# A conditioned low-rank linear kernel on one core: condition numbers read from DRAM for the first two tiles, and one residual sum and its loads moved in the opening

## What is computed

```python
y = jnp.einsum('bct,bcd->bdt', x, cond_weights[condition])
z = jnp.einsum('bsd,od->bso', y, W) + b
u = jnp.einsum('bsd,edr->ebsr', y, A)
m = jnp.einsum('ebsr,ero,e->bso', u, B, p_scores)
gamma = jnp.minimum(0.5 * norm(z) / (norm(m) + 1e-6), 1.0)
out = x + z + gamma * m
```

## Time and profile before

| what | value |
|---|---|
| median of three runs | 925.62 us (925.12 to 926.47) |
| the profiled execution | 925.62 us, of which the trace's span is 923.8 us |
| busy, share of the span | PE 99%, DVE 62%, ACT 39%, POOL 35% |
| PE's share of the chain that ended last | 93% |
| mean granted TensorE clock | 0.998 of full |
| data moved by DMA | 75.16 MB, 81 GB/s on average |

### The profile page before, as it was taken

The page is one execution under the profiler, slowest core; times in us unless marked ns, Lnnn a source line. Parts: engine busy times, 40 slices in busy tenths (PEclk is TensorE's granted clock), DMA queues, the critical chain, the costliest instruction groups (busy, mean ns, idle before and its releaser), DMA issues.

```text
span 923.8 us, 15176 instructions
## 1 busy us (share of the span) xinstructions
PE 911.9 (99%) x4884; PEld 786.3 (85%) x4884; DVE 575.9 (62%) x897; ACT 358.2 (39%) x695; POOL 319.5 (35%) x317
## 2 busy tenths in 40 slices
PE   8999999999999999999999999999999999999996
PEld 6888888888888888888888888888888888888885
DVE  5995656556565556565565655565655656555664
ACT  6653443324334333433343343334333433433342
POOL 0123443224433244432344332444323443324441
PEclk9999999999999999999999999999999999999999
DMA  8212221122221122211222211222112222122211
GB/s 292 81 70 95 81 85 69 47 94 94 71 93 46 71 94 75 90 66 50 94 94 71 93 45 73 94 71 94 61 56 94 94 71 93 40 77 94 72 46 68
DMA packets 32600, 75.16 MB, mean 81 GB/s; under 512 B 12745, under 2 KB 13770, under 8 KB 32586
## 3 DMA queue, kind: packets, MB, share of 16 engines
q1 hardware_dynamic: 32138, 74.43, 22.6%
q10 hardware_dynamic: 448, 0.56, 0.2%
HBM read 41.42 MB, written 33.55 MB: 81 GB/s over the span
## 4 chain that ended last, share of the span: by engine, by line
PE 93%; DVE 4%; DMA 1%; SPq 1%; issue 1%; ACT 0%; DVEq 0%
PE b_ps L853 36%; PE c_ps L853 18%; PE mix_ps L840 11%; PE u_ps L892 10%; PE m_ps L903 9%; PE a_ps L853 9%; DMA a_lo_raw<-in_L_ffn_A_dram 1%; SPq L266 1%; DVE w_lo L612 1%; DVE s_lo L642 0%; DVE y_lo L621 0%; DVE w_lo L576 0%; DVE w_lo_raw L595 0%; DVE w_lo_raw L581 0%; PE mix_ps L903 0%
## 5 line engine op out<-in xcount | busy, mean ns | idle before, releaser
L423 ACT CAST y_hi<-mix_ps 128x512 fp32r<-128x512 f32 x126 | 74.4, 592 | 309.3 <-PE mix_ps L840 309.3
L364 POOL TENSOR_TENSOR stats<-stats 128x1 f32<-128x1 f32 x32 | 18.8, 588 | 474.3 <-ACT squares L471 474.3
L642 DVE TENSOR_TENSOR s_lo<-s,s_hi 128x512 fp32r<-128x512 f32 x124 | 135.9, 1115 | 4.2
L840 PEld LDWEIGHTS mix_ps<-mixer,x_in 128*128 128x128 f32 x1008 | 122.2, 192 | 6.7 <-DMA x_in<-in_x_dram 1.0
L840 PE MATMUL mix_ps<-mixer,x_in 128*128 128x128 f32 x1008 | 122.9, 275 | 0.6 <-DVE y_lo L621 0.5
L436 ACT CAST s_hi<-s 128x512 fp32r<-128x512 f32 x124 | 76.6, 618 | 115.8 <-POOL s L338 93.7
L350 POOL TENSOR_TENSOR z<-z,x_in 128x512 f32<-128x512 f32 x61 | 79.2, 1299 | 116.7 <-ACT squares L452 116.7
L621 DVE TENSOR_TENSOR y_lo<-mix_ps,y_hi 128x512 fp32r<-128x512 f32 x126 | 86.4, 687 | 46.0 <-ACT s L429 39.6
L853 PE MATMUL b_ps<-w_hi,y_hi 128*128 128x512 f32 x256 | 100.1, 391 | 0.0
L853 PE MATMUL b_ps<-w_lo,y_hi 128*128 128x512 f32 x256 | 100.0, 391 | 0.0
L853 PE MATMUL b_ps<-w_hi,y_lo 128*128 128x512 f32 x256 | 99.6, 389 | 0.0
(11 more groups left out here) (120 smaller groups left out, 1842.5 us busy)
## 6 DMA issues: line engine op xcount, KB each, us to landing
x_in<-in_x_dram SPq DMA_DIRECT2D x64, 512.0 KB, 3.7
out_dram<-z SPq DMA_DIRECT2D x63, 512.0 KB, 2.7
w_lo_raw<-in_L_ffn_W_dram SPq DMA_DIRECT2D x8, 256.0 KB, 6.5
mixer<-in_L_cond_weights_dram SPq DMA_DIRECT2D x126, 16.0 KB, 2.1
w_hi_raw<-in_L_ffn_W_dram SPq DMA_DIRECT2D x6, 256.0 KB, 6.6
w_hi_raw<-in_L_ffn_W_dram ACTq DMA_DIRECT2D x2, 256.0 KB, 3.0
a_lo_raw<-in_L_ffn_A_dram SPq DMA_DIRECT2D x1, 512.0 KB, 7.9
b_lo_raw<-in_L_ffn_B_dram SPq DMA_DIRECT2D x1, 512.0 KB, 7.0
```

The costliest lines, as they stand in the source:

```text
L364: nc.gpsimd.tensor_tensor(stat(NORM_Z, 1), stat(Z_SQ, 1), half, ALU.pow).then_inc(norm_z_ready[1], 1)
L423: nc.scalar.copy(y_part(y_hi, r, h), source(h)).then_inc(y_hi_ready, 1)
L642: nc.vector.tensor_tensor(s_lo[:, n, :, :], s_raw(n), s_hi[:, n, :, :].bitcast(fp32), ALU.subtract).then_inc(s_lo_ready, 1)
L840: made = nc.tensor.matmul(source(h)[:, k, :], x_in[:, slot, (h * HC + k) * P:(h * HC + k + 1) * P], mixer[:, r, :], start=True, stop=True)
```

## The change

In the opening, the condition numbers of tiles 0 and 1 are no longer read from `cond_ids` in SBUF but straight from the input in DRAM; the DMA that fills `cond_ids` moves behind the loads of W12. SP and ACT therefore don't wait for it. ACT issues its small mixer DMAs and W11's first two chunks before the load of its activation table. The scaling of B by the scores moves from ACT to DVE. The bias difference `bias[:, 2]` is made later on DVE, between a split of T1 and the splits of S3 and S1. The square of z's upper half of tile 0 moves on ACT behind the squares of tile 1. The residual of tile 0 moves on DVE from before the splits of T4 to behind `add_p4_bias(1)`, and in SP's first half-step the load of tile 4 and of its mixers stands behind the loads of tile 5 and the store of tile 1, as in all later steps. Nothing inside the loop's steady part changes, save that `square_z11` names one semaphore less.

```diff
         def first_condition(engine, t, q):
             n = t * PER + q
-            return engine.value_load(cond_ids[0:1, n:n + 1], min_val=0, max_val=E - 1)
+            return engine.value_load(condition.rearrange("(o n) -> o n", o=1)[:, n:n + 1], min_val=0, max_val=E - 1)
...
-            sp.dma_start(cond_ids[:, :], condition.rearrange("(o n) -> o n", o=1)).then_inc(ids_loaded, 16)
             sp.dma_start(x_in[:, 0, :], x_tiles[0]).then_inc(x_loaded[0], 16)
             sp.wait_ge(mixer_zeroed, 1)
-            sp.wait_ge(ids_loaded, 16)
             sp.dma_start(first_mixer(0, 0), cond_block(first_condition(sp, 0, 0))).then_inc(mixer_loaded[0], 16)
...
             load_w(W12)
+            sp.dma_start(cond_ids[:, :], condition.rearrange("(o n) -> o n", o=1)).then_inc(ids_loaded, 16)
             load_w(W21)
...
-                    if first:
-                        sp.wait_ge(residual0_ready, 2)
-                        sp.dma_start(x_in[:, 0, :], x_tiles[4]).then_inc(x_loaded[0], 16)
-                        sp.wait_ge(mix_done, halves(2, 1))
-                        load_mixer(4, 0)
...
-                    if not first and not closing:
+                    if not closing:
                         sp.wait_ge(residual0_ready, 2 * p)
...
                 if not opening:
                     act.wait_ge(z12_squared, p)
-                    act.wait_ge(m_squared[1], p)
...
                 if opening:
-                    act.wait_ge(z12_squared, 1)
+                    act.wait_ge(z11_squared, 1)
...
-            act.dma_start(raw11[:, 0, :], w_blocks[W11][0]).then_inc(w_loaded[W11][0], 16)
+            act.wait_ge(mixer_zeroed, 1)
+            act.dma_start(first_mixer(0, 1), cond_block(first_condition(act, 0, 1))).then_inc(mixer_loaded[0], 16)
+            for k in range(2):
+                act.dma_start(raw11[:, k, :], w_blocks[W11][k]).then_inc(w_loaded[W11][k], 16)
+            act.dma_start(first_mixer(1, 1), cond_block(first_condition(act, 1, 1))).then_inc(mixer_loaded[1], 16)
             act.wait_ge(half_set, 1)
             nc.scalar.activation(table_out, half, ACT.Square).then_inc(table_loaded, 1)
-            act.wait_ge(mixer_zeroed, 1)
-            act.wait_ge(ids_loaded, 16)
-            act.dma_start(first_mixer(0, 1), cond_block(first_condition(act, 0, 1))).then_inc(mixer_loaded[0], 16)
-            act.dma_start(raw11[:, 1, :], w_blocks[W11][1]).then_inc(w_loaded[W11][1], 16)
-            act.dma_start(first_mixer(1, 1), cond_block(first_condition(act, 1, 1))).then_inc(mixer_loaded[1], 16)
...
-            act.wait_ge(bm_loaded, 16)
-            act.wait_ge(p_loaded, 16)
-            nc.scalar.activation(b_raw, b_raw, ACT.Copy, scale=p_col).then_inc(bm_scaled, 1)
...
-            square_z12(0, 0, z11_squared)
...
             square_m1(0, True)
+            square_z12(0, 0, m_squared[1])
...
+            dve.wait_ge(bm_loaded, 16)
+            dve.wait_ge(p_loaded, 16)
+            nc.vector.tensor_scalar(b_raw, b_raw, p_col, None, ALU.mult).then_inc(bm_scaled, 1)
             make_t3(0)
...
-            dve.wait_ge(z11_squared, 1)
-            dve.wait_ge(z12_squared, 1)
-            nc.vector.tensor_tensor(z0[:, 0, :], z0[:, 0, :], x_in[:, 0, :], ALU.add).then_inc(residual0_ready, 2)
             split_t(T4, 0)
...
             split_t(T3, 0)
             dve.wait_ge(bias_difference_ready, 1)
             add_p4_bias(1)
+            dve.wait_ge(z12_squared, 1)
+            nc.vector.tensor_tensor(z0[:, 0, :], z0[:, 0, :], x_in[:, 0, :], ALU.add).then_inc(residual0_ready, 2)
             split_t(T3, 1)
```

More of the change, by code:

```diff
@@ L735, in _ @@
             make_t1(1)
-            nc.vector.tensor_tensor(bias[:, 2, :], bias[:, 0, :], bias[:, 1, :], ALU.subtract
-                                    ).then_inc(bias_difference_ready, 1)
             dve.wait_ge(plain_done, 6)
@@ L772, in _ @@
             split_t(T1, 1)
+            nc.vector.tensor_tensor(bias[:, 2, :], bias[:, 0, :], bias[:, 1, :], ALU.subtract
+                                    ).then_inc(bias_difference_ready, 1)
             split_s(1, S3)
```

## The result

The changed kernel takes 942.56 us (938.20 to 942.97, four runs) against 925.4 us before: ratio 1.0173, 95% interval 1.0149 to 1.0196. It is slower by 17 us, where 11 were forecast; the time lies 2.6 us above the range. The profiled execution took 940.29 us, 2.3 less than the median.

The account below looks back on a forecast made before the run. PE was taken as the bound, busy without pause in the loop, so any standstill before it adds to the end. 9.1 us of stall and 1.9 of clock make 11.0 on 925.62: 936.6 us, range 933.0 to 940.0.

Parts of the forecast that it names:

- The stop before tile 4: PE waits for tile 4 and its mixers, so that mix starts at 66.0 instead of 56.44, 9.6 us later, 9.1 net.
- s: Cost of the scaling of B in DVE's list: 0.6 us, bounds 0.55 to 1.15.
- The landing: From the residual's end and tile 4's issue until its mixers have landed and PE can mix: 4.9 us.
- L: Time of one register load from DRAM, two per condition number: 0.8 us, between 0.28 and 1.3.
- d: How much later DVE's backlog begins, through SP's later DMA of A: 1.5 us, bounds 0 and 4.1.
- the forecast 61.1: End of tile 0's residual on DVE in us, from 59.03 + 0.6 + 1.5.
- Neither counts, because PE afterwards stops for tile 4 anyhow: PE's later start and ACT's table load in the opening cost nothing, as PE then waits less for tile 4.
- PE's late start: Tile 1's mix about 1 to 2 us later through the second mixer DMA, counted as nothing.
- The clock: PE's clock falls to 1.2 GHz in the pause before tile 4, a loss of 1.9 us, bounds 0 and 2.5.
- Rival 1: The stall before tile 4 without the clock's fall: 934.7 us, or 932.9 with d = 0 and short landing; chance 0.17.
- Rival 2: Slow register loads from DRAM, L = 1.3 and nothing absorbed: 940.0 us; chance of over 939: 0.12.
- Rival 3: Faster: tile 4 no later than its mix, PE loses its waits of 1.2 + 0.6 + 0.5 us: 923.3 us; chance 0.03.

Follow-up runs that it names:

- The move alone: The kernel before with only the residual of tile 0, tile 4's load and the square of z12 moved: 934.95 us, ratio 1.0099.
- the fill of the first pause: Changed kernel with residual and tile 4's load put back, plus 20 spare matmuls between the mixes of tiles 0 and 1: 930.74 us against 933.51 without.
- the DRAM loads alone: The kernel before with only the condition numbers of tiles 0 and 1 read from DRAM and the changed order of first issues: 932.59 us, ratio 1.0066.
- those four profiles: Changed kernel (942.56 us), the same again (941.19), and with 24 (940.08) or 34 (939.74) spare matmuls ahead of tile 4's mix.
- the move undone: Changed kernel with the residual of tile 0, the square it waits for and tile 4's load back at their old places: 933.51 us, ratio 1.0079.
- the last three kernels: The kernel before with the bias difference later on DVE (926.27 us); with it and tile 0's residual on GpSimd (926.13); the latter with tile 1 loaded earlier (927.24).
- the attempt above: The kernel before with the bias difference and the residual of tile 0 given from VectorE to GpSimd: 926.13 us, ratio 1.0002.

## Why the prediction was right or wrong

*The stop before tile 4* was right in place and chain: residual behind `add_p4_bias(1)`, issue of tile 4 within 0.02 us of its end, the mixer's DMA last, PE idle 8.2 us (7 to 10 were named). The move alone gave 9.1 us, and taking the residual up in DVE's list took 9.2 away again.

*s*, the scaling on DVE, was taken as 0.6; it occupies 0.67 us of the list, from its start at 26.87 to the next at 27.54. The Trainium skill ("VectorE: DVE Perf Modes", Mode 2×_2P) has fp32 `tensor_scalar` at twice the rate of `tensor_tensor`; 0.67 against 1.13 is 1.7 times the rate, near that. *The landing* was taken as 4.9 and measured 4.5.

*L and d were too small.* This is the first failed term. A register load from DRAM was put at 0.8, with both loads of a number alike and 1.3 as the upper bound, taken from a DMA's trip. The two aren't alike: the address takes 1.6 to 2.3 us, the number 0.5 to 0.8, together 2.3 to 2.8 instead of 1.6. SP came to W at 8.73 instead of 7.4, and DVE's backlog began 3.1 us late, not 1.5. The bound 2L = 2.6 held on SP and not on ACT. In DVE's list that is 1.6 us, of the 4.0 by which the residual ended later than the forecast 61.1.

*"Neither counts, because PE afterwards stops for tile 4 anyhow" was wrong.* This is the second failed term, and the reason for the missed range. I counted PE's late start as covered by PE's later pause. But the pause doesn't end at a fixed time: DVE's list waits for PE's first products and the residual stands in that list. The waits sum to 1.95 us in the profile (0.45 and 0.97 for products, 0.24 and 0.29 for ACT's copies of the mix behind them). With the 1.6 they make 3.5 of the residual's 4.0 us; the rest is the 0.07 of s and, at each of the four waits, some 0.08 by which DVE's rows otherwise overlap. The shorter landing gives 0.4 back, which leaves the 3.6 at tile 4's mix. This split is bookkeeping: the wait for `c_ps` ends with PE's product, so a list that began 1.6 us sooner would have waited longer and reached the residual at the same time (inferred from the waits; the rows show it for 0.36 us). What sets its time is PE's late start. That was put at 1 to 2 us and was 5.6 (16.34 against 10.75): 4.2 because ACT issues its second matrix only at 9.33 instead of 4.88, and 1.4 because tile 1's mix ran at half rate, which I had not looked for at all. The fixed 25.28 us behind the wait and the sum of the parts show the mechanism; the fill of the first pause shows what the half rate can cost there, 2.8 us in the execution compared.

*The clock* behind tile 4 was put at 1.9 and cost 2.1 in the trace. The Trainium skill ("TensorE: Matmul & The Clock Gate", Part 1) has the array fall to half rate when idle; the rows agree (0.50 in the pause before tile 4, 0.68 and 0.50 around tile 1 with the DRAM loads alone), and my failure was to apply it to one pause and not to the other. Rival 1 (no fall) is refuted.

*Rival 2*, slow loads, was the nearest case, at 940.0 with a chance of 0.12: right in kind, but its price lacked the way through PE. That it came within 0.3 us of the profiled execution was luck: it had d at 4.1, s at 1.15 and the landing at 5.2 where 3.1, 0.67 and 4.5 were measured, 2.2 us too much, and left out the 1.95 us of waits. In the profiled execution the sum is now closed: 69.62 - 56.44 = 13.2, plus 2.1 for the clock, less the wait of 0.5 at tile 5: 14.8 against 14.7 in the span. The further 2.3 us between the profiled execution and the median fit a later start of tile 1's mix, which was at 13.2, 14.4, 13.4 and 13.9 us in those four profiles, and at 15.2 in the one with the move undone, and a longer stretch at half rate behind it (1.4 to 2.8 us in the seven profiles); no unprofiled run can show it, so this is argued and not shown. Why that wait varies stays open: its DMA travels among those of W11 and W12, and no run put it ahead of them.

*Rival 3* was rightly small. Its premise that PE's early waits can be won was itself too kind: the last three kernels went for them and won nothing. In the first the list was as long as before, in the second it came out no shorter, since DVE ran slower beside GpSimd, and in the third the first mixers landed later.

## What to carry to other kernels

A late start isn't covered by a later pause of the same engine if what ends the pause waits, through another engine's list, for that start: trace the pause's end back before counting anything as hidden. When an instruction that frees a buffer is moved in a list that runs without idleness, its new time is the sum of the list, and it must lie a full load (here 4.5 us) ahead of the buffer's next use. A pause can cost more than its length: behind the two here PE's work ran at half rate for a while, which took another 2.1 us at tile 4 and 1.4 to 2.8 us at tile 1.

## What the runs showed of the hardware

- A register load from DRAM took 1.6 to 2.3 us for the address and 0.5 to 0.8 us for the number behind it; from SBUF it took 0.28 to 0.48. Reading a number from DRAM took 2.3 to 2.8 us in all each time, the second number of an engine no faster than the first.
- TensorE fell to 1.2 GHz in the pause of 8 us. In all seven profiles with the DRAM loads and no spare work before tile 1, its mix ran at half rate behind waits of 2.8 to 5.4 us: 3.1 to 3.4 us up to the first product, not 1.8. The granted clock shows the fall in the pause or just behind it in five of them; in the other two (the move undone, 24 spare matmuls) the column reads 1.00 against the spacing, and in four of the seven tile 0's mix was already slow (3.7 us instead of 2.0), behind waits of 1.1 to 1.6 us. With 24 spare matmuls before tile 4 it fell although only the last 2.7 us were idle, and with 34 (0.4 us idle) it stayed at 2.4 GHz; each is one profile.
- A DVE sum or difference of two SBUF tensors beside a GpSimd one took up to 1.1 us longer: in the changed kernel the bias difference 1.78 us instead of 0.68, beside a sum on GpSimd. Before, the same GpSimd sum met two splits of s at 54.29, which took 2.38 us where they take 1.28 now, so the move of the bias difference itself cost nothing. In these two cases and beside GpSimd's sums in the attempt above, the DVE operations ended, within 0.2 us, when they would have if the one that met GpSimd's had begun as that ended: here 60.43 against 59.88 + 0.68 = 60.56. DVE's rows, and GpSimd's:

```profile
58.65 1.78 DVE L761 TENSOR_TENSOR bias<-bias 128x512 f32<-128x512 f32 x1
60.34 1.28 DVE L632 TENSOR_TENSOR s_lo<-s,s_hi 128x512 fp32r<-128x512 f32 x2
```

```profile
58.43 1.45 POOL L345 TENSOR_TENSOR z<-z,x_in 128x512 f32<-128x512 f32 x1 [6.13 <-ACT squares L446]
```
